# Two-layer transformer with routed experts: second-layer attention from stacked halves in one stage, experts written out

## The reference

```python
xn = layernorm(x)
x  = x + L0_attn(xn) + L0_ffn(xn)      # 16 heads of 128, causal; 32 experts, top 4, inter 96
xn = layernorm(x)
x  = x + L1_attn(xn) + L1_ffn(xn)      # 4 heads kept, dim 16, causal, softmax, biases
# L1_ffn: rmsnorm, 32 experts with w13 (256 x 256) and w2 (128 x 256), top 4,
#         a shared expert, and its own residual
```

## Time and profile before

| | us |
|---|---|
| median of 3 runs | 1405.49 |
| lowest, highest | 1400.72, 1407.36 |
| the profiled execution | 1400.54 |
| its span in the trace | 1398.2 |
| mean granted clock of PE | 0.913 |
| PE busy in the span | 1185.2 (85%) |
| DVE, ACT, POOL busy | 794.4, 541.2, 500.1 |

### The profile page before, as it was taken

One profiled execution on the slowest core, in us unless ns is written; L12 is line 12 of the kernel. 1 busy time (PEld: TensorE's weight loads), 2 busy tenths in 40 slices (PEclk: granted clock), 3 DMA queues, 4 the chain that ended last, 5 costly groups with the idle time before them and its releaser, 6 DMA issues. The chain is left out here.

```text
span 1398.2 us, 21769 instructions
## 1 busy us (share of the span) xinstructions
PE 1185.2 (85%) x5610; PEld 840.6 (60%) x5613; DVE 794.4 (57%) x2002; ACT 541.2 (39%) x1532; POOL 500.1 (36%) x479
## 2 busy tenths in 40 slices
PE   5679999999689997788899999697749899986167
PEld 5446667777567776455567778554325788862023
DVE  4867876664045544899987773473224455542147
ACT  2336665554023333455555552210213333331022
POOL 0667765552000000666655550324740000007710
PEclk9879999999889999999999999898659999995569
DMA  9332322223454554322222210201930444433311
GB/s 364 155 102 89 93 92 74 74 69 139 139 146 155 158 154 129 97 75 76 76 72 73 76 50 1 71 27 64 384 128 0 139 156 157 157 120 103 111 42 38
DMA packets 107080, 154.70 MB, mean 111 GB/s; under 512 B 13712, under 2 KB 87696, under 8 KB 104720
## 3 DMA queue, kind: packets, MB, share of 16 engines
q1 hardware_dynamic: 67072, 95.07, 21.4%
q0 software_dynamic: 12288, 33.57, 7.5%
q10 hardware_dynamic: 27648, 25.18, 5.2%
HBM read 97.01 MB, written 56.75 MB: 110 GB/s over the span
## 5 line engine op out<-in xcount | busy, mean ns | idle before, releaser
L793 POOL TENSOR_TENSOR parts<-wq,parts 128x256 fp32r<-128x256 f32 x64 | 48.9, 764 | 399.7 <-ACT parts L1038 399.7
L1163 PE MATMUL bank<-big_a,probsT 128*128 x768 | 182.3, 360 | 0.4 <-issue 0.2
L1047 ACT ACTIVATE probs<-bank,negmax 128x256 f32<-128x256 f32 (+3 forms) x256 | 134.7, 536 | 123.3 <-DVE negmax L962 120.7
L1235 DVE COPY probsT<-bank 128x256 f32<-128x256 f32 x192 | 81.4, 424 | 172.1 <-PE bank L1147 172.1
L854 PE MATMUL bank<-kT,qT 128*128 128x256 f32 (+3 forms) x512 | 173.0, 460 | 0.0
L1163 PEld LDWEIGHTS bank<-big_a,probsT 128*128 128x128 f32 x768 | 140.2, 192 | 22.8 <-issue 8.6
L870 PE MATMUL bank<-const,probs 128*128 128x128 f32 x640 | 128.5, 274 | 28.2 <-DVE probs L974 28.2
L886 PE MATMUL bank<-probsT,big_b 128*128 128x512 f32 (+3 forms) x512 | 149.0, 434 | 0.0
L1477 POOL DMA_INDIRECT big_a<-ys_dram,slot_r x64 | 61.5, 960 | 241.1 <-POOLq L149 221.9
L962 DVE TENSOR_REDUCE negmax<-bank 128x1 f32<-128x256 f32 (+3 forms) x256 | 113.7, 485 | 48.1 <-PE bank L856 46.9
L838 PE MATMUL bank<-parts 128*128 128x512 f32 x256 | 115.0, 484 | 20.0 <-POOL parts L793 15.4
(11 more groups left out here) (195 smaller groups left out, 2099.5 us busy)
## 6 DMA issues: line engine op xcount, KB each, us to landing
probs<-xs_dram SPq DMA_DIRECT2D x192, 128.0 KB, 2.1
ys_dram<-work ACTq DMA_DIRECT2D x192, 128.0 KB
work<-khT_dram SPq DMA_DIRECT2D x64, 256.0 KB
xs_dram<-big_a SPq DMA_DIRECT2D x12, 1024.0 KB, 20.3
wq<-in_wq SPq DMA_DIRECT2D x64, 128.0 KB
big_a<-in_gu SPq DMA_DIRECT2D x1, 8192.0 KB
big_a<-in_gu SPq DMA_DIRECT2D x1, 6144.0 KB
big_b<-in_dn SPq DMA_DIRECT2D x1, 4096.0 KB
```

The source lines that it names most:

```text
L1047: nc.scalar.activation(s.probs[:, par, ROW_AT[i]:ROW_AT[i] + (i + 1) * P], s.ps[bank][:, at:at + (i + 1) * P], ACT.Exp, bias=s.negmax[:, p ...
L1163: mm = nc.tensor.matmul(s.ps[2 + j % 2][:, 0:W], rowsT[:, j % 2, k * P:(k + 1) * P], gu[:, k, bass.ds(e * W, W)], start=k == 0, stop=k == ...
L1235: v.tensor_copy(rowsT[:, j % 2, :], s.ps[j % 2][:, 0:EMB]).then_inc(rowsT_ready, 1)
```

## The change

**Route stage of layer 1.** `take` writes one batch's queries and keys to a shared pair of buffers (q_full, k_full) in place of xnT. ACT copies them to a type that PE multiplies in one pass (fp32r), rounding them to a high half (`split_high`); POOL subtracts to get the low half (`split_low`), one pair before the scatters and one behind every eight. SP stores the halves to DRAM as stacks, six stores of 256 KB a batch: queries high, low, high; keys high, high, low, so that a stack's product over 96 rows is high x high + low x high + high x low. From the second batch on `take` waits for the low halves of the batch before. Two loads of 2 MB of expert weights stand ahead on SP's queue.

```diff
+                sp.dma_start(s.gu1[:, 1, EARLY_GU1:], gu[:, 1, EARLY_GU1:]).then_inc(early_in, 16)
+                for b in range(BATCH):
+                    q_hi, q_lo, k_hi, k_lo = (a.bitcast(F32) for a in parts1(s, b))
+                    stack = d["stack1"][b]
+                    sp.wait_ge(high_ready, 2 * b + 2)
+                    sp.dma_start(stack[0, :, 0], q_hi).then_inc(stored[b % 2], 16)
+                    sp.dma_start(stack[2, :, 0], q_hi).then_inc(stored[b % 2], 16)
+                    sp.dma_start(stack[0, :, 1], k_hi).then_inc(stored[b % 2], 16)
+                    sp.dma_start(stack[1, :, 1], k_hi).then_inc(stored[b % 2], 16)
+                    sp.wait_ge(low_ready, 2 * b + 2)
+                    sp.dma_start(stack[1, :, 0], q_lo).then_inc(stored[b % 2], 16)
+                    sp.dma_start(stack[2, :, 1], k_lo).then_inc(stored[b % 2], 16)
...
+                    nc.gpsimd.tensor_tensor(q_lo, q_full, q_hi.bitcast(F32), ALU.subtract).then_inc(low_ready, 1)
+                    nc.gpsimd.tensor_tensor(k_lo, k_full, k_hi.bitcast(F32), ALU.subtract).then_inc(low_ready, 1)
...
+                split_low(0)
                 pool.wait_ge(slots_done, 1)
-                for t in range(EARLY_TILES):
-                    scatter_tile(nc, s, d, 1, t, moved)
+                for b in range(1, BATCH):
+                    for t in (2 * b - 2, 2 * b - 1):
+                        scatter_tile(nc, s, d, 1, t, moved)
+                    split_low(b)
...
+                    if b >= 2:
+                        act.wait_ge(stored[b % 2], 16 * 6 * (b // 2))
+                    a(q_hi, q_full, ACT.Copy).then_inc(high_ready, 1)
+                    act.wait_ge(rotated, b + 1)
+                    a(k_hi, k_full, ACT.Copy).then_inc(high_ready, 1)
...
-                cols = slice(b * SEQ, (b + 1) * SEQ)
-                for i, (dst, bank, bias) in enumerate(((s.xnT[:, 0, cols], Q_BANK, bqs), (s.rope_a, KA_BANK, bka),
+                if b:
+                    dve.wait_ge(low_ready, 2 * b)
+                for i, (dst, bank, bias) in enumerate(((q_full, Q_BANK, bqs), (s.rope_a, KA_BANK, bka),
                                                        (s.rope_b, KB_BANK, bkb))):
...
-                link(v.tensor_tensor(s.xnT[:, 1, cols], s.rope_a, s.rope_b, ALU.add))
+                v.tensor_tensor(k_full, s.rope_a, s.rope_b, ALU.add).then_inc(rotated, 1)
```

```diff
 SLOT_TILES = 96
...
-        def tiles(eng, step, tail):
-
-            for i in range(UNROLL):
-                step(i, i)
-            with eng.Fori(0, (N - 2 * UNROLL) // STEPS) as r:
-                for j in range(STEPS):
-                    step(STEPS * r + (UNROLL + j), (UNROLL + j) % STEPS)
-            for i in range(N - UNROLL, N + tail):
-                step(i, i % STEPS)
+        N = USED_TILES
...
+                    pe.wait_ge(x_in[i % UNROLL], 16 * (i // UNROLL + 1))
...
-            tiles(pe, step, 2)
...
+            for i in range(N + 2):
+                if i < N:
+                    e = expert_of(i)
+                    for k in range(KC):
+                        gate_up(i, k, e)
+                        if i + 2 < N:
+                            turn_rows(i + 2, k)
+                if i + 2 < N:
+                    read_expert(i + 2)
+                if 1 <= i < N + 1:
+                    turn_hidden(i - 1)
+                if i >= 2:
+                    down(i - 2)
...
-                if not known(i) or i + 2 < N:
-                    rowsT_out(i + 2, (j + 2) % UNROLL)
-                if not known(i) or i < N:
-                    hidden(i, j)
-                if not known(i) or 1 <= i < N + 1:
-                    hidT_out(i - 1, (j - 1) % UNROLL)
...
+            for i in range(N + 2):
+                if i < N:
+                    hidden(i)
+                if i + 2 < N:
+                    rowsT_out(i + 2)
+                if 1 <= i < N + 1:
+                    hidT_out(i - 1)
```

```diff
+                for part in range(3):
+                    sp.dma_start(s.stacks[part * HP1:(part + 1) * HP1, u % STACKS1].bitcast(F32),
+                                 d["stack1"][b, part, h * HP1:(h + 1) * HP1].rearrange("l a n -> l (a n)")
+                                 ).then_inc(stack_in[u % STACKS1], 16)
...
+            for u in range(NU):
...
+                    sp.dma_start(s.gu1[:, :, a:z], gu[:, :, a:z]).then_inc(w_in, 16)
...
+                if u + STACKS1 < NU:
+                    sp.wait_ge(producted, u + 1)
+                    load_stack(u + STACKS1)
...
+            def products(u):
+                q, k = stack(u)
+                for n, (bank, tiles) in enumerate(SCORES1_T):
+                    if u:
+                        pe.wait_ge(exped, len(SCORES1_T) * (u - 1) + n + 1)
+                    for i, (j, at) in enumerate(tiles):
+                        w = (ROWS - j) * P
+                        mm = nc.tensor.matmul(s.ps[bank][:, at:at + w], k[:, j * P:(j + 1) * P], q[:, j * P:],
+                                              start=i == 0, stop=False)
...
+                    mask(s.ps[bank], 0, len(tiles) * P, False, True)
+
+            def shift(u):
+                pe.wait_ge(shift_ready, u + 1)
+                for bank, tiles in SCORES1_T:
+                    for i, (j, at) in enumerate(tiles):
+                        w = (ROWS - j) * P
+                        mm = nc.tensor.matmul(s.ps[bank][:, at:at + w], s.onesr[:], s.shift[:, u % 2, j * P:],
+                                              start=False, stop=i == len(tiles) - 1)
+                    mm.then_inc(score_ready, 1)
...
+                for n, (j, at) in enumerate(PROBS1_T):
+                    pe.wait_ge(exped, len(SCORES1_T) * u + EXPED1[j])
+                    mm = nc.tensor.matmul(HEAD_BANK[:, j * P:], values[b][:, j], probsT[u % 2][:, at:at + (ROWS - j) * P],
+                                          start=n == 0, stop=n == ROWS - 1)
...
+                nc.tensor.matmul(SUM_BANK[:, :], sums, heads[b % 2], start=True, stop=True).then_inc(summed, 1)
...
+            for u in range(NU):
+                if u + 1 < NU:
+                    scores(u + 1)
+                products(u)
+                after_batch(u)
+                shift(u)
+                if u:
+                    weigh(u - 1)
+            weigh(NU - 1)
+            for u in range(NU + 1, NU + H1):
+                after_batch(u)
...
+                v.tensor_tensor(s.shift[:, u % 2].rearrange("p (i n) -> p i n", i=ROWS),
+                                s.c("ident").unsqueeze(1).to_broadcast([P, ROWS, P]),
+                                s.negmax[:, u % 2].unsqueeze(2).to_broadcast([P, ROWS, P]), ALU.mult).then_inc(shift_ready, 1)
+
+            def normalise(b):
+                dve.wait_ge(summed, b + 1)
+                v.reciprocal(recip, SUM_BANK[:, :]).then_inc(recip_ready, 1)
+                dve.wait_ge(recip_ready, b + 1)
+                v.tensor_tensor(heads[b % 2], heads[b % 2], recip, ALU.mult).then_inc(normed, 1)
...
+                    nc.scalar.activation(probsT[u % 2][:, at:at + w], s.ps[bank][:, 0:w], ACT.Exp).then_inc(exped, 1)
```

```diff
+        @block.sync
+        def _(sp):
+            out = d["out"].rearrange("(t p) e -> p t e", p=P)
+            for g in range(TILES // 2):
+                sp.wait_ge(x_added, 2 * TOPK * (g + 1))
+                sp.dma_start(out[:, 2 * g:2 * g + 2], s.x[:, 2 * g:2 * g + 2]).then_inc(y_stored, 16)
+            sp.wait_ge(y_stored, 16 * TILES // 2)
...
+            for t in range(TILES):
+                dve.wait_ge(gathered[t], 16 * TOPK)
+                for k in range(TOPK):
+                    if k:
+                        dve.wait_ge(x_added, TOPK * t + k)
+                    nc.vector.scalar_tensor_tensor(out=s.x[:, t, :], in0=gath[:, t * TOPK + k],
+                                                   scalar=s.weight[:, t, k:k + 1], in1=s.x[:, t, :],
+                                                   op0=ALU.mult, op1=ALU.add).then_inc(x_added, 1)
...
+    out["bv1"][0, D1::HP1], out["wo1"][D1] = 1.0, w["L1_attn_bo"]
...
+    out["sums1"] = ((lane[:, None] % HP1 == D1) & (lane[:, None] // HP1 == lane[None, :] // HP1)).astype(np.float32)
...
+        attention_block1(nc, s, d)
         expert_block(nc, s, d, 1)
-        attention_block1(nc, s, d, [2, 3], "combine")
+        combine_block1(nc, s, d)
```

506 lines of the change are left out of this document (241 added, 265 removed).

## The result

The changed kernel takes 1362.95 us (median of 4 runs, 1362.06 to 1364.80) against 1404.86 (4 runs): a ratio of 0.9706, with a 95% interval of 0.968 to 0.9732. The profiled execution took 1363.39, with a span of 1362.2 and a mean granted clock of 0.911. The forecast was 1367.

What follows compares the result with a forecast made beforehand. It took PE's late signals under POOL's trains to bound layer 1's route and attention stages, and PE's sequencer the experts. -22 - 5 + 0 + 43 - 52 = -36 gave 1364.5 to 1369.5, forecast 1367 us, range 1324 to 1394.

Steps and rivals of the forecast that it cites:

- Slow signals: Layer 1's route and attention stages: PE's signals arrive late, some 8.3 us apart, after 13 us of POOL's scatters or gathers.
- The +43: Layer 1's single attention stage: 16 units at 4.7 us, PE's signals late until about 55 us; 147.7 us against 104.5.
- The -52: Last stage: only 64 gathers and additions remain, PE signals nothing; 93 us against 145.7 (-47 to -55).
- The reciprocal: Attention stage, DVE, 128x512 per batch: 3.3 us, just fitting, so only the last batch's is on the path.
- Experts: Both layers: PE's sequencer bounds the loop; writing it out gives pitches of 1.43 and 1.61, -22 and -5 us.
- Layer 0's term: Layer 0's experts: pitch from 1.646 to 1.43 us over 95 tiles and one tile less, -22 us.
- The claim that the order moves nothing: Experts: placing PE's turns between the two gate matmuls gains nothing else.
- Rival (b): Expert stages: written-out code starves for instructions, 0.2 us more a tile than the loop, kernel about 1432 us; chance 0.08.
- The value taken, 0: Layer 1's route stage: no net change taken, between -4 and +8 us.
- the lower end, -4: Layer 1's route stage: 10.2 us trains with 2.4 us gaps may stay below 13 us, ending slow signals; -4 us.
- Rival (a): Attention stage: no slow signals, so 104.4 us, 0 instead of +43, kernel about 1324 us; chance 0.18.
- the rule of three cases: Route and two attention stages of layer 1: only PE's signals are late under POOL's trains, prompt in the first 13 us.

Runs made afterwards that it cites:

- e_loop: Changed kernel with the expert stages of before (hardware loop, 96 tiles, old order); 1349.22 us on the chip where before takes 1304.6.
- e_order: Changed kernel, experts still written out, but PE's turns behind both gate matmuls and DVE's copy ahead of its product; 1365.91 us where before takes 1406.8.
- t_16: Changed kernel with POOL pausing 2.6 us behind 16 and 32 scatters only in the attention stage; 1347.35 us (one run) where before takes 1406.8.

## Why the prediction was right

**Slow signals, attention stage and last stage.** Right, by mechanism and size, on the chips where before takes 1400: they are a matter of POOL's unbroken train (148.5 against 117.6 us with four pauses), they begin some 13 us into it (975.50 in a train from 959.86), and they move with it. What the change does is to hold 16 units where it held eight, and to leave PE nothing to signal under the 64 gathers. The +43 measured +43.8: a pitch of 4.76 where I took 4.7, one weighing done by 1016, as assumed, and 11.1 us of tail (from the end of the last weigh, 1096.2) where I had 9.5. First scores at 9.9 us, where I had 7, cost nothing, since what follows them waits for the scatters to end. The -52 measured -54.0, in a stage of 90.3 us against 93. The terms I gave for it add up to 92.3; the first gather starts 0.7 us into the stage where I had 2.2, the pitch is 1.276 where I had 1.26, and behind the last start come 9.2 us where the terms have 10.8, among them 4 for the store and the end that no row had shown.

**The reciprocal** of 128x512 takes 3.36 us, and 3.3 was read from the slope of the earlier trace rows. "VectorE: DVE Perf Modes" of the Trainium skill ("First, the fixed hardware budget"), by which it was an estimated 4.3, is above the measurement; in kind it holds, since the product of the same shape takes 0.69. It was hidden in three batches of four, as the sum had it: PE's next matmuls for the output follow without a wait.

**Experts.** Layer 1 right: 1.606 a tile against 1.61. Layer 0's term was a little too large: 1.454 against 1.43, 95 x 0.024 = 2.3 of the 2.5 us. The row behind it was weaker than I took it to be: the down products of before start 1.46, 1.42, 1.56 and 1.80 us apart, 1.42 is the shortest, and the product at 397.67 is already the loop's. That PE's queue with its extra instructions and the loop bound both layers is borne out by `e_loop` and `e_order` (written out, but in the old order, the pitch is 1.496 and 1.604) and by the waits for "issue" (in layer 1 they were 2.9 us from 1120 to 1240 before, and none from 1140 to 1260 now). How much of it is address arithmetic, how much the waits on registers and how much the branch, no run separates. The claim that the order moves nothing was wrong by 3 to 4 us in layer 0. Rival (b), starving for instructions, did not occur: pitches of 1.454 and 1.606 leave no room for it, as "Runtime: NRT & Kernel Launch" ("Instruction fetch mechanics") in the Trainium skill would have it.

**Route stage.** The value taken, 0, was at fault by 4.4 us, and the lower end, -4, is about what came. Trains of eight with two subtractions between them stayed prompt, as that end supposed; it is the first experiment on the pause, done by the change itself.

**The total** is closer than its parts. -36 against -36.1 is luck: experts 0 brought 2.5 us less than forecast, the route stage and the last stage 4.4 and 2 more, the other stages differ by up to 1, and the misses cancel.

**Rival (a)** is what one chip shows: stages of 112.7 to 113.6 us, not for the reason that (a) gave but with the same train. Its price was some 9 us too low: the start and the tail account for about half. The rest isn't located; the granted clock was 0.50 over the first 23 us of `e_loop`'s stage.

**What the prediction didn't see** is that the rule of three cases depends on the chip as well. It called the cause unknown, and took it to belong to the program. On the chip without late signals the sum would read: experts -22.7 by `e_loop`, and everything else +44.6 (1326.5 - 1304.6 + 22.7). My explanation, an estimate, is that eight units more in front of the experts cost their own 8 x 4.76 = 38 us there, and that the last stage, with POOL's 64 gathers in any case, gives little back when its eight units go. The kernel before was not traced on that chip, so this split is not shown. A forecast for both chips would have had to name two times.

What makes PE's signals late under such a train, and why one chip of those used shows nothing of it, stays open. The intervals of 3 to 8 us between late signals, and their running on behind the train's end (5 us in the changed kernel, where the last scatter's instruction ends at 1010.8 and the last late maximum starts at 1015.53, and 2 to 3 in `t_16`), would fit something that fills and drains; no run shows what.

## To carry over

A wait whose waited-for instruction has long ended in the trace is a cost of its own: look for what else runs in all such places, here a train of 16 or more indirect DMAs on POOL, and break the train before rebuilding the work beneath it. Four pauses of POOL in one stage were worth 33 us here, and pauses in all three trains, with the new experts, brought the old structure to 0.926 of its time, where the new structure brought 0.971. And a gain that rests on a stall is worth what the stall is worth on the chip in question: profile the kernel before on each chip at hand.
